# A periodic drain in the scatter queue of a fused attention and mixture-of-experts kernel

## The chip, the cores and the metric

The kernel runs on one core of one Trainium2 chip. The metric is the device time of one execution in microseconds. Three runs of the kernel before took 1343.55, 1356.92 and 1354.8 us; their median is 1354.8 us.

## What is computed

The input is x of shape (4, 512, 256), 2048 rows of 256 floats. Four residual layers follow each other, each on a layernorm of its input:

```
x = x + attn_a(layernorm(x))     # 32 query heads of 8, 8 key/value heads, rope, causal
x = x + ffn(layernorm(x))        # the layer called "f" in the kernel
x = x + attn_b(layernorm(x))     # differential attention, 16 heads, causal
x = x + ffn(layernorm(x))        # the same weights; the layer called "h"
```

The part that matters is ffn. Each of the 2048 rows goes to a shared expert (width 352) and to 4 of 16 routed experts (width 176):

```
scores  = softmax(xt @ Wg.T)                     # 16 experts
topi    = top 4 experts within the best 2 of 4 groups
h       = silu(xt @ W1[e]) * (xt @ W3[e]);  y = sum over chosen e of score * (h @ W2[e])
z       = (silu(xt @ Ws1.T) * (xt @ Ws3.T)) @ Ws2.T
out     = y + z
```

## The kernel before, in words

**Tiling.** The 2048 rows are 16 tiles of 128 rows (NT = 16). In a ffn layer, DVE works out in two halves of 8 tiles each (the function assign, L1308) which slot of a table in DRAM, x_slots, each (row, choice) pair goes to; its slot numbers are in slot_i. There are 16 x 4 = 64 such pairs of a tile and a choice (NT * TOPK). For each of them, POOL issues one indirect DMA, here called a scatter: 128 rows of 265 floats (the 256 features, the slots, the scores and the row number) go from y_sb to 128 places of x_slots (L687). Scatter n carries tile n // 4, choice n % 4.

**What limits the scatters.** Scatters of even number count their landing on one semaphore, scat0, those of odd number on another, scat1. Before scatter n, POOL waits until scatter n - 2 has landed (L686), so at most two are under way. Scatters 0 to 31 need the first half of the slots, 32 to 63 the second half.

**What waits for the scatters.** Once scatters 0 to 39 have landed (EARLY_T * TOPK = 40; L503 and L504), SyncE starts to load the gathered rows, one tile of 128 slots after another (load, L468), 72 tiles in all (NJ), eight ahead of their use. Before tile 24 it waits for all 64 (L511 to L513). Before that, SyncE itself has filled the ends of the experts' regions with zero rows (16 small DMAs, L498) and has stored x as the start of the accumulator (store_x, L489), three of four batches.

**The expert stage.** PE turns two loaded tiles at a time (turn_in, L1971), multiplies them by the first-layer weights of their experts (L1996), turns the result (L2003) and multiplies by the second-layer weights (L2029 to L2034). ACT and DVE sit between (L896 to L905, L1463, L1471). DVE scales the result into one of eight buffers, yt (L1480), and POOL sends each result back with an indirect DMA that adds to y_f or y_h in DRAM (result_out, L703).

**POOL's order in a ffn layer.** Scatters 0 to 51 stand one after another, with one wait for the second half of the slots before scatter 32. Then come the results of the 72 tiles, and after each of the first six results, two of the last 12 scatters. Everything on POOL is in this written order.

**Beside the scatters.** While the scatters run, PE computes the shared expert (L1938, L1948), with ACT's silu (L896) and DVE's product and sum (L1429, L1421).

Attention, weights and the return of the result (L525 to L534) are not touched.

Of the kernel before, what the change touches and what calls it, by code (L numbers as in the profile page):

```python
# [26 lines left out]
NT = B * TB  # L27
# [26 lines left out]
TOPK = 4  # L54
# [46 lines left out]
def build(nc, ins, out):  # L101
    ctx = ExitStack()
    with ctx:
# [3 lines left out]
        def sem(name):  # L107
            return ctx.enter_context(nc.semaphore(name))
# [159 lines left out]
        def sm(name):  # L268
            if name not in S:
                S[name] = sem(name)  # L270
            return S[name]
# [65 lines left out]
        def past(f, n):  # L337

            return n if f == "h" else 0
# [341 lines left out]
        def pool_ffn(pool, f):  # L681

            def scatter(n):
                t, k = n // TOPK, n % TOPK
                if n >= 2:
                    pool.wait_ge(sm(f"scat{n % 2}"), 16 * (n // 2 + past(f, NT * TOPK // 2)))  # L686
                pool.indirect_dma_start(x_slots, bass.IndirectOffsetOnAxis(ap=slot_i[:, t, k:k + 1], axis=0),  # L687
                                        y_sb[:, t, :], None).then_inc(sm(f"scat{n % 2}"), 16)

            outs = [(j, h) for j in range(NJ) for h in range(1 + (j in MIX))]  # L690

            def scatter_out(s):


                if s >= ACCS:
                    i, h = outs[s - ACCS]
                    if h == 0:
                        pool.wait_ge(sm(f"store{i % XR}"), 16 * (i // XR + 1 + past(f, NJ // XR)))
                    else:
                        pool.wait_ge(sm("store_second"), 16 * (MIX.index(i) + 1 + past(f, MIXED)))  # L700
                j, h = outs[s]
                to = j if h == 0 else NJ + MIX.index(j)
                pool.indirect_dma_start(y_acc[f][s % ACCS], bass.IndirectOffsetOnAxis(ap=dest[:, to:to + 1], axis=0),  # L703
                                        yt[:, j % XR, :], None, compute_op=ALU.add)\
                    .then_inc(sm(f"store{j % XR}" if h == 0 else "store_second"), 16)

            def result_out(j):
                pool.wait_ge(sm("e_dest"), j // 4 + 1 + past(f, NJ // 4))
                pool.wait_ge(sm("e_y_ev"), j + 1 + past(f, NJ))
                if j == 0:  # L710
                    pool.wait_ge(sm("acc_x"), 16 * B * (1 + past(f, 1)))
                scatter_out(outs.index((j, 0)))
                if j in MIX:
                    scatter_out(outs.index((j, 1)))

            pool.wait_ge(sm("e_slots"), 1 + past(f, 2))
            pool.wait_ge(sm("cleared"), 16 * 23)
            for n in range(TH * TOPK):
                scatter(n)
            pool.wait_ge(sm("e_slots"), 2 + past(f, 2))  # L720
            for n in range(TH * TOPK, EARLY_T * TOPK + LATE_FIRST):
                scatter(n)
            late = range(EARLY_T * TOPK + LATE_FIRST, NT * TOPK)
            for j in range(NJ):
                result_out(j)
                for n in late[2 * j:2 * j + 2]:
                    scatter(n)
# [1418 lines left out]
```

## Time and profile before

| what | value |
|---|---|
| median of three runs | 1354.8 us |
| time of the profiled execution | 1349.85 us |
| its span | 1348.1 us |
| PE busy | 1144.7 us (85%) |
| DVE busy | 873.5 us (65%) |
| POOL busy | 689.1 us (51%) |
| ACT busy | 541.6 us (40%) |
| mean granted clock of TensorE, share of full speed | 0.934 |

The span is what the profiler recorded from first to last instruction; the device time of the same execution is 1.75 us longer. A busy share is the mean over all stages, and says little about one stage. Layer f runs its scatters from 388 us on and its experts until about 648 us; layer h from 1037 us and until about 1314 us. All times in the views are counted from the start of the span. "DMA_INDIRECT" on POOL is the time in which POOL makes the descriptors of a scatter; the data moves after it.

### The profile page before, as it was taken

How to read it: one execution, taken by the hardware profiler on the slowest of the kernel's cores; microseconds unless marked ns; L12 is line 12 of the kernel's file. 1: busy time of each engine (PE TensorE's matmuls, PEld its weight loads, DVE VectorE, ACT ScalarE, POOL GpSimd, SP SyncE). 2: the span in 40 equal slices, each digit the busy share in tenths (PEclk: the TensorE clock that was granted, in tenths of full speed). 3: DMA queues.
4: the chain of work that ended last, by engine and by line, in shares of the span. 5: the costliest groups of instructions: out<-in, count | busy, mean ns of one | idle time of the engine just before them, and what ended most of it. 6: DMA issues, size and time to landing. Idle time of an engine off the chain costs nothing.

```text
span 1348.1 us, 26055 instructions
## 1 busy us (share of the span) xinstructions
PE 1144.7 (85%) x8706; PEld 614.0 (46%) x8706; DVE 873.5 (65%) x2067; ACT 541.6 (40%) x846; POOL 689.1 (51%) x841
## 2 busy tenths in 40 slices
PE   6888999998899699999288899999779859999990
PEld 2343444342655366566154344444246435665650
DVE  5688899981576145555388899999568523554543
ACT  2124777779431122222032577777844001222210
POOL 4452344544036577767552454545521652787671
PEclk9897999999889799999699899999988978999995
DMA  4424433320825479987754321221062345898868
GB/s 144 144 86 126 122 109 121 106 64 2 287 72 149 150 183 164 158 156 113 192 178 143 108 61 53 62 50 50 3 255 48 113 129 144 168 159 161 153 91 262
DMA packets 145875, 169.84 MB, mean 126 GB/s; under 512 B 20240, under 2 KB 130768, under 8 KB 145232
## 3 DMA queue, kind: packets, MB, share of 16 engines
q1 hardware_dynamic: 115856, 128.79, 32.7%
q0 software_dynamic: 29184, 38.36, 16.7%
q8 instruction: 73, 1.20, 0.4%
q10 hardware_dynamic: 704, 1.02, 0.2%
q14 instruction: 58, 0.48, 0.1%
HBM read 93.29 MB, written 76.18 MB: 126 GB/s over the span
## 4 chain that ended last, share of the span: by engine, by line
PE 57%; DVE 18%; issue 6%; DMA 6%; ACT 6%; POOL 2%; SPq 2%; another core or an unknown queue 1%; POOLq 0%; ACTq 0%; DVEq 0%
PE pair_ps L1996 11%; PE o_ps L1761 9%; ACT arena L849 4%; DVE nm L1123 4%; PE pair_ps L2029 4%; DMA x_slots<-y_sb,slot_i 3%; DVE bm L1123 3%; PE pair_ps L2032 2%; PE t_ps L1787 2%; PE pair_ps L1711 2%; PE pair_ps L1592 2%; PE pair_ps L1691 2%; PE pair_ps L1716 2%; PE pair_ps L2003 2%; PE pair_ps L1686 2%
## 5 line engine op out<-in xcount | busy, mean ns | idle before, releaser
L849 ACT ACTIVATE arena<-pair_ps 128x1024 f32<-128x1024 f32 x320 | 322.9, 1024 | 130.6 <-PE pair_ps L1686 75.9
L625 POOL TENSOR_SCALAR_AFFINE_SELECT arena<-arena 128x512 f32<-128x512 f32 (+1 forms) x320 | 175.0, 547 | 241.4 <-ACT arena L849 240.9
L1123 DVE TENSOR_REDUCE nm<-pair_ps 128x2 f32<-128x1024 f32 (+1 forms) x192 | 232.6, 1222 | 33.4 <-PE pair_ps L1735 29.5
L687 POOL DMA_INDIRECT x_slots<-y_sb,slot_i x128 | 123.6, 966 | 168.0 <-DVE slot_i L1321 94.0
L1761 PE MATMUL o_ps<-arena 128*9 128x512 f32 (+7 forms) x2048 | 176.8, 440 | 4.2 <-POOL arena L625 4.1
L1996 PE MATMUL pair_ps<-arena 128*128 x512 | 168.6, 471 | 2.5 <-ACT arena L900 2.5
L1123 DVE TENSOR_REDUCE bm<-pair_ps 128x8 f32<-128x1024 f32 x128 | 155.3, 1217 | 4.1 <-PE pair_ps L1735 1.0
L703 POOL DMA_INDIRECT y_h<-xnT,dest x80 | 125.3, 1567 | 58.6 <-DVE xnT L1480 31.4
L703 POOL DMA_INDIRECT y_f<-xnT,dest x80 | 124.6, 1558 | 42.0 <-issue 21.2
L1463 DVE TENSOR_TENSOR arena<-arena,pair_ps 128x128 f32<-128x128 f32 x144 | 41.4, 288 | 116.6 <-ACT arena L905 77.1
L1996 PEld LDWEIGHTS pair_ps<-arena 128*128 128x128 f32 x512 | 93.8, 195 | 43.9 <-issue 6.3
L905 ACT ACTIVATE arena<-pair_ps 128x176 f32<-128x176 f32 x144 | 45.5, 317 | 138.6 <-PE pair_ps L1996 86.9
L1480 DVE TENSOR_SCALAR xnT<-pair_ps,slot_w 128x256 f32<-128x256 f32 x144 | 64.9, 481 | 45.5 <-PE pair_ps L2034 15.9
L1938 PE MATMUL pair_ps<-arena 128*128 128x512 f32 (+1 forms) x192 | 90.3, 614 | 0.0
L1735 PE MATMUL pair_ps<-c_b 64*128 64x128 bf16 (+1 forms) x1280 | 85.0, 210 | 0.0
L1735 PEld LDWEIGHTS pair_ps<-c_b 64*128 64x128 bf16 x1280 | 60.8, 98 | 33.5 <-issue 4.2
L1711 PE MATMUL pair_ps<-arena 48*128 48x512 bf16 x256 | 51.2, 394 | 22.7 <-ACT arena L849 17.9
L896 ACT ACTIVATE sil<-pair_ps 128x512 f32<-128x512 f32 (+1 forms) x24 | 14.3, 595 | 128.3 <-PE pair_ps L1938 66.3
L1686 PE MATMUL pair_ps<-arena 51*128 51x512 bf16 x256 | 51.2, 395 | 15.3 <-DVE bm L1123 7.3
L1761 PEld LDWEIGHTS o_ps<-arena 128*9 128x9 f32 (+1 forms) x2048 | 38.9, 93 | 53.3 <-issue 30.7
L2029 PE MATMUL pair_ps<-arena 128*128 x224 | 59.5, 388 | 0.5 <-DVE arena L1471 0.5
L900 ACT ACTIVATE arena<-t_ps 128x512 f32<-128x512 f32 x36 | 21.5, 597 | 86.2 <-PE t_ps L1971 73.8
(275 smaller groups left out, 2012.8 us busy)
## 6 DMA issues: line engine op xcount, KB each, us to landing
arena<-x_slots SPq DMA_DIRECT2D x128, 132.5 KB
arena<-in_w SPq DMA_DIRECT2D x4, 2816.0 KB, 18.9
arena<-q_a SPq DMA_DIRECT2D x64, 96.0 KB
arena<-q_b SPq DMA_DIRECT2D x64, 96.0 KB
y_f<-hw SPq DMA_DIRECT2D x11, 512.0 KB, 2.9
y_h<-hw SPq DMA_DIRECT2D x11, 512.0 KB, 2.9
arena<-in_w SPq DMA_DIRECT2D x2, 2048.0 KB, 17.4
arena<-y_f SPq DMA_DIRECT2D x8, 512.0 KB
```

The source lines that it names most:

```text
L625: pool.affine_select(p, p, pattern, ALU.is_ge, 0.0, base=0, channel_multiplier=-1)\
L687: pool.indirect_dma_start(x_slots, bass.IndirectOffsetOnAxis(ap=slot_i[:, t, k:k + 1], axis=0), y_sb[:, t, :], None).then_inc(sm(f"scat{n ...
L703: pool.indirect_dma_start(y_acc[f][s % ACCS], bass.IndirectOffsetOnAxis(ap=dest[:, to:to + 1], axis=0), yt[:, j % XR, :], None, compute_op ...
L849: act.activation(p_ring[:, U % RING, :], pair_ps[:, pair_at("T", n, u)].rearrange("p a c -> p (a c)"), ACT.Exp, scale=SCALE).then_inc(sm(" ...
L1123: dve.tensor_reduce(dst, src, X, ALU.max, negate=not 2 <= u < 4).then_inc(sm("t_max_done"), 1)
L1686: mm = pe.matmul(ps, k_of(s, g, h, KM, 0, P), q_of(g, h, KM, 0, T), start=True, stop=True, skip_group_check=True)
L1711: pe.matmul(ps, q_of(g, h, KQ, 3 * P, T), k_of(s, g, h, KQ, 0, T), start=True, stop=False, skip_group_check=True)
L1735: mm = pe.matmul(blocks[:, :, 64 * half:64 * half + 64], mask_h[lo:lo + 64, half * P:half * P + P], ident_b[lo:lo + 64, lo:lo + 64].unsque ...
L1761: mm = pe.matmul(o_ps[32 * h:32 * h + vw, T - c:T], v_all[:, g, TB * b + j, v0:v0 + vw], p_ring[:, U % RING, a:a + c], start=j == 0, stop= ...
L1938: mm = pe.matmul(st_ps[0:m, k % 2, 512 * a:512 * a + 512], ws13[:, a, e, r:r + m], xnT_all[:, e, b * T:(b + 1) * T], start=e == 0, stop=e ...
L1996: mm = pe.matmul(s_ps[:, j % 2, 0:2 * INTER], xgT[:, j // 2 % 2, j % 2, c, :], w13[:, c, ds(e, 1), :].rearrange("p a i -> p (a i)"), start ...
L2029: pe.matmul(st_ps[:, h, 512:512 + E], hsT[:, h, :], w2[:, 0, ds(e, 1), :].rearrange("p a d -> p (a d)"), start=True, stop=False, skip_grou ...
```

## The change

Before scatters 8, 16, 24, 32, 40, 48 and 56 of each ffn layer, POOL also waits until the scatter just before has landed. So nothing of the scatters is under way when one of these is issued. That is 7 waits in each of the two layers. No instruction is added on another engine, no data moves differently, and POOL's order stays the same.

```diff
                 t, k = n // TOPK, n % TOPK
                 if n >= 2:
                     pool.wait_ge(sm(f"scat{n % 2}"), 16 * (n // 2 + past(f, NT * TOPK // 2)))
+                if n > 0 and n % 8 == 0:
+                    pool.wait_ge(sm(f"scat{(n - 1) % 2}"), 16 * ((n + 1) // 2 + past(f, NT * TOPK // 2)))
                 pool.indirect_dma_start(x_slots, bass.IndirectOffsetOnAxis(ap=slot_i[:, t, k:k + 1], axis=0),
                                         y_sb[:, t, :], None).then_inc(sm(f"scat{n % 2}"), 16)
```

For n = 8, scatters 1, 3, 5 and 7 count on scat1, and (8 + 1) // 2 = 4 landings are asked for: all of them.

## Rows read from the trace of the kernel before

**Rows 1.** The page's chain of work that ended last: shares by line.

```profile
PE pair_ps L1996 11%; PE o_ps L1761 9%; ACT arena L849 4%; DVE nm L1123 4%; PE pair_ps L2029 4%; DMA x_slots<-y_sb,slot_i 3%; DVE bm L1123 3%; PE pair_ps L2032 2%; PE t_ps L1787 2%; PE pair_ps L1711 2%; PE pair_ps L1592 2%; PE pair_ps L1691 2%; PE pair_ps L1716 2%; PE pair_ps L2003 2%; PE pair_ps L1686 2%
```

**Rows 2.** The chain in layer f: start us, us, what.

```profile
430.03 4.93 DMA x_slots<-y_sb,slot_i
...
437.95 5.19 DMA x_slots<-y_sb,slot_i
...
451.84 2.67 DMA x_slots<-y_sb,slot_i
454.52 0.03 SPq L504
...
465.06 2.66 DMA arena<-x_slots
...
467.82 0.44 PE t_ps L1971 x2
```

**Rows 3.** POOL's timeline, layer f: scatters 8, 9, 12, 16, 17, 24, 25, 32, 33.

```profile
401.89 0.95 POOL L687 DMA_INDIRECT x_slots<-y_sb,slot_i  x1 [2.21 <-DMA x_slots<-y_sb,slot_i]
403.15 0.96 POOL L687 DMA_INDIRECT x_slots<-y_sb,slot_i  x1 [0.30 <-issue]
...
407.48 0.96 POOL L687 DMA_INDIRECT x_slots<-y_sb,slot_i  x1 [0.64 <-DMA x_slots<-y_sb,slot_i]
...
413.60 0.96 POOL L687 DMA_INDIRECT x_slots<-y_sb,slot_i  x1 [0.69 <-issue]
415.06 0.96 POOL L687 DMA_INDIRECT x_slots<-y_sb,slot_i  x1 [0.50 <-issue]
...
425.60 0.96 POOL L687 DMA_INDIRECT x_slots<-y_sb,slot_i  x1 [0.52 <-DMA x_slots<-y_sb,slot_i]
427.30 0.96 POOL L687 DMA_INDIRECT x_slots<-y_sb,slot_i  x1 [0.74 <-DMA x_slots<-y_sb,slot_i]
...
439.76 0.96 POOL L687 DMA_INDIRECT x_slots<-y_sb,slot_i  x1 [0.86 <-DMA x_slots<-y_sb,slot_i]
443.40 0.96 POOL L687 DMA_INDIRECT x_slots<-y_sb,slot_i  x1 [2.68 <-DMA x_slots<-y_sb,slot_i]
```

**Rows 4.** SyncE's waits in 380 to 480 us: total, times, longest.

```profile
SPq L504 <- DMA x_slots<-y_sb,slot_i: 16.0, 1, 16.0
```

**Rows 5.** Windows in layer f: busy us of each engine, granted clock, DMA share, GB/s.

```profile
455.00:460.00 5.00, 1.23 (x4) 0.58 (x4) 0.00 (x0) 0.00 (x0) 3.52 (x4) 0.50 0.55 160
460.00:465.00 5.00, 3.90 (x8) 2.29 (x8) 1.20 (x7) 0.91 (x2) 2.81 (x4) 0.50 0.76 219
```

**Rows 6.** Timelines, layer f: last scatter and first result on POOL, tile 24's load on SyncE.

```profile
474.84 1.61 POOL L703 DMA_INDIRECT y_f<-xnT,dest  x1 [2.29 <-issue]
...
500.60 0.96 POOL L687 DMA_INDIRECT x_slots<-y_sb,slot_i  x1 [0.30 <-issue]
...
508.74 1.39 SPq L468 DMA_DIRECT2D arena<-x_slots  x2
```

**Rows 7.** POOL's waits in 470 to 650 us: total, times, longest.

```profile
POOL y_f L703 <- DVE xnT L1480: 13.0, 12, 2.4
```

**Rows 8.** Timelines, layer h: SyncE, then POOL (scatter 41, first result), PE, ACT.

```profile
1057.02 41.42 SPq L498 DMA_DIRECT2D x_slots<-x_slots  x16
1101.34 11.24 SPq L489 DMA_DIRECT2D y_h<-x_sb  x3
...
1098.58 0.96 POOL L687 DMA_INDIRECT x_slots<-y_sb,slot_i  x1 [0.64 <-DMA x_slots<-y_sb,slot_i]
...
1138.69 1.62 POOL L703 DMA_INDIRECT y_h<-xnT,dest  x1 [19.89 <-DVE xnT L1480]
...
1092.00 2.05 PE L1948 MATMUL t_ps<-arena,hw 128*128 128x256 f32 x4 [18.12 <-DVE x_sb L1421]
...
1124.60 0.63 PE L1971 MATMUL t_ps<-c_f,arena 128*128 128x128 f32 x4 [1.81 <-issue]
...
1084.62 0.60 ACT L896 ACTIVATE sil<-pair_ps 128x512 f32<-128x512 f32 x1 [18.63 <-issue]
```

## The prediction

> **What bounds the kernel now.** I read the page's chain of waits first. PE work has the largest shares, and the scatters of the dispatch hold 3% of the span [rows 1]. That is enough to ask where they stand. The same chain in order of time answers it: between 388 and 455 us nearly every link is a scatter or POOL's issue of the next, and the last of them, scatter 39, leaves at 451.84 and lands 2.67 us later. SyncE is released at 454.52, its loads follow, and the experts' chain on PE begins with a load that lands at 467.7 [rows 2]. SyncE's waits say the same: it had done its own work 16.0 us before and stood at L504 for the scatters alone [rows 4]. PE is idle meanwhile: 1.23 of 5 us busy in 455 to 460, 3.90 of 5 in the next window, at the lower level of its clock (0.50 granted, 1.2 GHz) in both [rows 5]. So in layer f, what delays scatter 39 delays everything after it.
>
> In layer h the same scatters end nothing. Scatter 41 starts at 1098.58, released by the landing of 39, so 39 had landed by then. SyncE issues its three stores until 1101.34 + 11.24 = 1112.6, loads then, and PE turns the first tile at 1124.60 when its shared expert is done [rows 8]. The slack is 1112.6 - 1098.6 = 14 us at SyncE.
>
> **The change, part by part.** The added wait makes scatter n leave when n - 1 has landed, and not n - 2. Where before scatter n + 1 was held by exactly that landing, its own start tells when n could go now. From the starts [rows 3]:
> - n = 8: 403.15 - 401.89 = 1.26 us later at most. Scatter 9 left after 0.96 us of descriptors and a 0.30 us pause, the shortest spacing in the rows, so it was not held. Scatter 7 had landed by then; the price is 0 to 1.26, and I take 0.6.
> - n = 16: 415.06 - 413.60 = 1.46 us.
> - n = 24: 427.30 - 425.60 = 1.70 us.
> - n = 32: 443.40 - 439.76 = 3.64 us, behind the long landing of scatter 31 (5.19 us, [rows 2]).
>
> That is what the even scatter loses. The odd one behind it can now follow at the shortest spacing, 1.26 us, and loses just that; its loss at n = 32 is 443.40 + 1.26 - 443.40 = 1.26 as well. Scatter 39 is odd and is the one waited for. Its loss before any recovery is 0.6 + 3 x 1.26 = 4.4 us.
>
> Recovery: pairs that leave 1.26 us apart turn round a little faster than pairs evenly spaced. From scatter 8 to 12, started in close pairs, a pair took (407.48 - 401.89) / 2 = 2.8 us; from 16 to 24, evenly spaced, (425.60 - 413.60) / 4 = 3.0 us [rows 3]. With 0.2 us for some three pairs behind each of the two drains that break an even spacing (16 and 24), 1.2 us come back. **Layer f, start of the experts: 4.4 - 1.2 = about +3.2 us.** PE's clock adds nothing: it is already at 0.50 across the whole idle stretch [rows 5], and a longer idle leaves it there.
>
> The bounds: below, 0 for each drain, if the landing of n - 1 comes in fact right behind that of n - 2; the long landings (4.93 and 5.19 us, rows 2) may also be due to SyncE's stores at that moment and be met by other scatters now. Above, 4 us for each drain, the longest landing of the rows, 5.19 us, with a 0.26 us release in place of the 1.45 us pace: 16 us in all.
>
> **Drains 40 and 48** lie behind the point that SyncE waits for. What stands behind them on POOL is scatters to 51, then the results. The first result starts at 474.84 after 2.29 us of idle time [rows 6]. With all six drains scatter 51 is 3.2 + 2 x 1.26 = 5.7 us later, the first result's data 3.2 us later, so POOL's lag of 2.5 us nearly fits in that idle time. What is left is covered by the 13.0 us in which POOL waits for DVE's results later in the stage [rows 7], and by the eight yt buffers. If that cover were gone, the price would be some 1 us.
>
> **Drain 56** stands two results further on, with a result of 1.6 us of POOL's time between scatters 55 and 56; by then 55 has landed or nearly so: 0 to 1 us on POOL, 0 on the end. All 64 scatters are wanted before tile 24's load at 508.74; scatter 63 starts at 500.60 [rows 6] and, with the 2.67 us of a landing, is home at 503.3, 5.4 us ahead. It moves by 5.7 to 7, the load by 3.2, so 1.6 us or more are left.
>
> **Layer h**: four drains, at 4.4 us, fit in 14 us of slack. POOL waits 19.89 us for its first result at 1138.69 [rows 8], so drains 40 and 48 are hidden too. Zero; if the cover of 14 us went, 3.2 us as in f.
>
> The sum is +3.2 us on the profiled execution: 1349.85 + 3.2 = 1353.1 us. That execution is 4.95 us under the median of the runs shown; on the median the same sum is 1358.0. I give the middle of the two, **1355.5 us**. The runs shown lie 13.4 us apart, so a change of this size hardly shows in the time. About 1%, 13.5 us, is what a measurement here can tell from no change.
>
> **The rivals.**
> - *Drains under load, slower.* The drain exposes a whole landing, and the landings beside SyncE's zero rows and stores are the long ones, 4.93 and 5.19 us [rows 2]. If the drains of layer f meet such landings, each costs 4 us: 1349.85 + 16 = 1365.9 us. It passes the 1% where a drain costs over 13.5 / 4 = 3.4 us. For it: two of the long landings are among scatters 27 to 31, right before drain 32. Against it: no scatter from 16 to 25 shows one, and drain 32 pays only once the stall that scatter 33 paid already. The Trainium skill, "DMA: Bandwidth & Descriptors", section "Latency and other measured facts", speaks for this rival: it gives access to HBM 0.2 us on average and 2 us at high load, as the main part of a transfer's fixed cost. By it four loaded drains would cost 4 x 1.8 = 7.2 us more, an estimate from that page; this trace agrees that landings vary (2.67 to 5.19 us), but shows the long ones to be few. Chance 0.10.
> - *The idle gap in layer h shrinks, faster.* ACT starts its silu at 1084.62 after 18.63 us in which nothing that the profile shows held it, and PE stands for 18.12 us until 1092.00 [rows 8]. If this is a fetch of instructions held up behind DMA traffic, a queue emptied now and then might let it through. PE would then end its shared expert up to 18 us sooner. SyncE would not follow that far: its fills are issued until 1057.02 + 41.42 = 1098.4, the stores take 11.24 us more, and a load 2.66 us to land [rows 2, 8], so PE's first turn could come at 1112.3 in place of 1124.60. The most that can be won is 12 us: 1349.85 + 3.2 - 12 = 1341.0 us; with half of it 1347. Against it: between drains the traffic is the same. The Trainium skill, "Runtime: NRT & Kernel Launch", section "Instruction fetch mechanics", says that the sequencers stream their code in blocks by a queue of their own and that this is mostly hidden; by it there would be nothing to win. The trace neither names the 18.63 us a fetch nor excludes it. Chance 0.12.
> - *The waits cost nothing.* The landing of n - 1 comes with that of n - 2, or the stalls are met elsewhere: 1349.9 us. For it: only scatter 8. Chance 0.10.
> - *The forecast*, +1 to +7 us, has the remaining 0.68.
>
> **How the numbers follow.** The range reaches down almost to the second rival's 1341 and up to the first's 1365.9, with a little for the difference of the bases: 1342 to 1367 us. Faster by over 1% needs more than the whole gap's gain or a low draw of the runs: 0.06. Slower by over 1% is the first rival with a little for what I don't see: 0.11. Within 1%: 0.83.
>
> **What would show each step right or wrong.** In the trace after, scatters 8, 16, 24 and 32 of layer f should start about 2.7 us behind the one before, and the next 1.26 us behind. From scatter 0's start to the release at L504 it should take 66.3 + 3.2 = 69.5 us, and PE's first tile should follow as now. SyncE in layer h should still end its stores some 12 us ahead of PE's first turn. The forecast is wrong if drains meet 5 us landings, if the pace between drains changes, if the gap in layer h has another length, or if POOL's lag reaches DVE's result buffers.

## The result

| | changed | before |
|---|---|---|
| median of 20 runs each, same chip | 1363.95 us (1356.88 to 1370.63) | 1351.65 us (1343.55 to 1361.78) |
| ratio, 95% interval | 1.009 (1.0068 to 1.0112) | |
| profiled execution | 1358.44 us | 1349.85 us |
| its span | 1356.7 us | 1348.1 us |

The change costs 12.3 us, 0.9%. That lies within 1%, though the interval reaches 1.12%, and 1363.95 lies within the range of 1342 to 1367. But the sum of the forecast was +3.2 us, and its likeliest case ended at +7. The size was wrong, and what follows is mostly about that. Here and below, medians are over all runs, while a ratio and its interval compare only the runs within 1.5% of the fastest of their kernel, which makes a difference in set 1 alone.

### The profile page after: what moved, and what is told of

Its sections match the earlier page's. It is cut to its first block, busy times and chain, and to the rows that moved or that the text cites. A ratio compares the mean times of both kernels' runs of the same rounds, so it can differ in the third digit from the quotient of the medians.

```text
span 1356.7 us, 26067 instructions
## 1 busy us (share of the span) xinstructions
PE 1144.0 (84%) x8706; PEld 610.8 (45%) x8706; DVE 872.1 (64%) x2067; ACT 542.0 (40%) x846; POOL 691.1 (51%) x841
## 4 chain that ended last, share of the span: by engine, by line
PE 54%; DVE 16%; DMA 12%; ACT 6%; issue 6%; POOL 2%; SPq 2%; another core or an unknown queue 1%; POOLq 0%; ACTq 0%; DVEq 0%
PE pair_ps L1998 11%; PE o_ps L1763 9%; DMA x_slots<-y_sb,slot_i 9%; ACT arena L851 4%; DVE nm L1125 4%; PE pair_ps L2031 4%; DVE bm L1125 3%; PE pair_ps L2034 2%; PE t_ps L1789 2%; PE pair_ps L1713 2%; PE pair_ps L1594 2%; PE pair_ps L2005 2%; PE pair_ps L1693 2%; PE pair_ps L1718 2%; PE pair_ps L1688 2%
## 5 line engine op out<-in xcount | busy, mean ns | idle before, releaser
L851 ACT ACTIVATE arena<-pair_ps 128x1024 f32<-128x1024 f32 x320 | 323.1, 1025 | 131.2 <-PE pair_ps L1688 76.5
L1482 DVE TENSOR_SCALAR xnT<-pair_ps,slot_w 128x256 f32<-128x256 f32 x144 | 65.0, 481 | 46.2 <-PE pair_ps L2036 14.6
L1713 PE MATMUL pair_ps<-arena 48*128 48x512 bf16 x256 | 51.6, 397 | 22.6 <-ACT arena L851 18.4
L1973 PE MATMUL t_ps<-c_f,arena 128*128 128x128 f32 x144 | 25.2, 295 | 36.5 <-DMA arena<-x_slots 36.5
```

What stands on the lines that cost most here:

```text
L851: act.activation(p_ring[:, U % RING, :], pair_ps[:, pair_at("T", n, u)].rearrange("p a c -> p (a c)"), ACT.Exp, scale=SCALE).then_inc(sm(" ...
L1713: pe.matmul(ps, q_of(g, h, KQ, 3 * P, T), k_of(s, g, h, KQ, 0, T), start=True, stop=False, skip_group_check=True)
```

## The profile after

The chain of waits on the profile's page gives the first hint. The scatters had 3% of the span in it [rows 1] and now have 9%:

```profile
PE pair_ps L1998 11%; PE o_ps L1763 9%; DMA x_slots<-y_sb,slot_i 9%; ACT arena L851 4%; DVE nm L1125 4%; PE pair_ps L2031 4%; DVE bm L1125 3%; PE pair_ps L2034 2%; PE t_ps L1789 2%; PE pair_ps L1713 2%; PE pair_ps L1594 2%; PE pair_ps L2005 2%; PE pair_ps L1693 2%; PE pair_ps L1718 2%; PE pair_ps L1688 2%
```

9% of 1357 us is some 120 us, and the scatters to number 39 of one layer take 70. So they now end the time in both layers, where before it was layer f alone. (Lines from 687 on have moved by two.)

POOL's timeline of the changed kernel in layer f: start, duration, and in brackets the idle time ahead. The rows are scatters 8, 16 to 18, 20, 24, 26, 30, 32, 39 and 51, and the first result. They answer to [rows 3] and [rows 6].

```profile
400.59 0.96 POOL L689 DMA_INDIRECT x_slots<-y_sb,slot_i  x1 [2.49 <-DMA x_slots<-y_sb,slot_i]
...
414.60 0.96 POOL L689 DMA_INDIRECT x_slots<-y_sb,slot_i  x1 [2.78 <-DMA x_slots<-y_sb,slot_i]
415.87 0.96 POOL L689 DMA_INDIRECT x_slots<-y_sb,slot_i  x1 [0.30 <-issue]
417.60 0.96 POOL L689 DMA_INDIRECT x_slots<-y_sb,slot_i  x1 [0.77 <-DMA x_slots<-y_sb,slot_i]
...
420.88 0.96 POOL L689 DMA_INDIRECT x_slots<-y_sb,slot_i  x1 [1.05 <-DMA x_slots<-y_sb,slot_i]
...
428.92 0.96 POOL L689 DMA_INDIRECT x_slots<-y_sb,slot_i  x1 [2.55 <-DMA x_slots<-y_sb,slot_i]
...
433.44 0.96 POOL L689 DMA_INDIRECT x_slots<-y_sb,slot_i  x1 [2.30 <-DMA x_slots<-y_sb,slot_i]
...
441.93 0.96 POOL L689 DMA_INDIRECT x_slots<-y_sb,slot_i  x1 [3.41 <-DMA x_slots<-y_sb,slot_i]
...
446.59 0.96 POOL L689 DMA_INDIRECT x_slots<-y_sb,slot_i  x1 [2.43 <-DMA x_slots<-y_sb,slot_i]
...
456.42 0.96 POOL L689 DMA_INDIRECT x_slots<-y_sb,slot_i  x1 [0.30 <-issue]
...
476.02 0.96 POOL L689 DMA_INDIRECT x_slots<-y_sb,slot_i  x1 [2.41 <-DMA x_slots<-y_sb,slot_i]
...
482.76 1.62 POOL L705 DMA_INDIRECT y_f<-xnT,dest  x1 [0.30 <-issue]
```

Each drain is there: scatters 8, 16, 24, 32 wait 2.4 to 2.8 us. The pace before scatter 16 does not break, but its start is 414.60 - 410.86 = 3.74 us behind scatter 15, which left at 410.86. The chain of waits says what these 3.74 us are (start, us, what):

```profile
410.86 2.97 DMA x_slots<-y_sb,slot_i
...
413.87 0.73 issue
```

Scatter 15 takes 2.97 us to land, and POOL then needs another 0.73 us in which the profile shows nothing that it waits for. All four drains of layer f have these 0.73 us. Behind the long landings of the kernel before it was 0.26 us: 437.95 + 5.19 = 443.14, and scatter 33 starts at 443.40 [rows 2, 3]. Scatters 26 and 30, which have no drain, wait long too (2.30 and 3.41 us): the two stalls that before met scatters 29 and 33 now meet others. From scatter 0's start (388.27 before, 386.59 after) to scatter 39 it takes 69.8 us in place of 63.6.

POOL's waits from 380 us to scatter 51, total, times and longest, after and then before:

```profile
POOL x_slots L689 <- DMA x_slots<-y_sb,slot_i: 37.4, 27, 3.4
```

```profile
POOL x_slots L687 <- DMA x_slots<-y_sb,slot_i: 26.6, 33, 2.8
```

The waits put down to a landing add up to 10.8 us more. From scatter 0 to scatter 51 it takes 94.9 us in place of 83.3, so six drains cost 11.6 us, 1.9 us each. SyncE's wait at L504 in layer f, 16.0 us before [rows 4], and the same in layer h, where before it never stood for a scatter:

```profile
SPq L504 <- DMA x_slots<-y_sb,slot_i: 22.1, 1, 22.1
...
SPq L504 <- DMA x_slots<-y_sb,slot_i: 24.7, 1, 24.7
```

On PE, the second turn of a pair of slot tiles (L2003 before, L2005 now) marks each of the 36 pairs of a layer. These are pairs 0 and 9 of layer f, before:

```profile
469.16 0.54 PE L2003 MATMUL pair_ps<-c_f,arena 128*128 128x128 f32 x3 [0.90 <-issue]
...
513.16 0.49 PE L2003 MATMUL pair_ps<-c_f,arena 128*128 128x128 f32 x3
```

and after, with two stalled ones between:

```profile
473.35 0.54 PE L2005 MATMUL pair_ps<-c_f,arena 128*128 128x128 f32 x3 [0.90 <-issue]
...
494.21 0.49 PE L2005 MATMUL pair_ps<-c_f,arena 128*128 128x128 f32 x2 [1.09 <-DVE arena L1465]
...
514.42 0.50 PE L2005 MATMUL pair_ps<-c_f,arena 128*128 128x128 f32 x2 [1.17 <-DVE arena L1465]
...
524.01 0.49 PE L2005 MATMUL pair_ps<-c_f,arena 128*128 128x128 f32 x3
```

These nine pairs take 50.7 us after and 44.0 before; the other 26 take 131.2 to 131.6 us in every kernel here. So the experts start late and then run slowly for nine pairs. This second loss is one that the forecast had put at nothing. What causes it in this trace is not shown. The profile puts no wait of DVE between 470 and 530 us down to the landing of a result, so nothing in it points at the result buffers. The chain of waits runs instead through stretches whose releaser the profile does not know, the longest of them this one:

```profile
504.39 4.88 another core or an unknown queue
```

It ends with ACT's copy of a turn that PE had finished at 504.83 (first PE's row, then ACT's):

```profile
504.17 0.66 PE L1973 MATMUL t_ps<-c_f,arena 128*128 128x128 f32 x4
```

```profile
509.29 0.60 ACT L902 ACTIVATE arena<-t_ps 128x512 f32<-128x512 f32 x1 [4.90 <-remote]
```

ACT takes up ready work 4.5 us late here. Set 1 has the same in layers without the drains that could explain it.

In layer h, POOL's scatter 0 and 39, SyncE's stores and its first load, and PE's first turn now stand so (to be held against [rows 8]):

```profile
1048.48 1.06 POOL L689 DMA_INDIRECT x_slots<-y_sb,slot_i  x1 [46.14 <-DVE slot_i L1323]
...
1120.97 0.96 POOL L689 DMA_INDIRECT x_slots<-y_sb,slot_i  x1 [0.32 <-DMA x_slots<-y_sb,slot_i]
...
1090.50 8.24 SPq L489 DMA_DIRECT2D y_h<-x_sb  x3
...
1124.29 1.49 SPq L468 DMA_DIRECT2D arena<-x_slots  x2
...
1126.88 0.66 PE L1973 MATMUL t_ps<-c_f,arena 128*128 128x128 f32 x2 [17.93 <-DMA arena<-x_slots]
```

The idle gap of 18 us in the shared expert is gone, the stores are out at 1098.7, and the load now waits for scatter 39. PE waits 17.93 us for it. The two profiled executions then add up like this; each row is worked out from the starts of scatter 0 and of pairs 0 and 9 in both traces.

| where the 8.6 us of the profiles arise | us |
|---|---|
| layer f starts earlier (386.59 against 388.27) | -1.7 |
| f, scatter 0 to pair 0: 86.8 against 80.9 | +5.9 |
| f, nine pairs: 50.7 against 44.0 | +6.7 |
| f's pair 9 to h's scatter 0 | +0.6 |
| h, scatter 0 to pair 0: 89.1 against 95.9 | -6.8 |
| h, nine pairs: 48.2 against 44.3 | +3.9 |

Whether the waits brought back the 6.8 us in layer h, the experiments had to tell.

## The experiments

Three sets, each on one chip; kernels of a set share their runs of the kernel before. That kernel's medians show how chips differ: 1360.57 us (1342.76 to 1385.03) in set 1, 1331.65 us (1326.12 to 1337.11) in set 2, 1329.78 us (1324.29 to 1335.04) in set 3. Ratios are compared inside a set. Each diff is against the changed kernel, unless it says otherwise.

### Set 1: which layer, which drains, and four scatters under way

f_only keeps the waits of layer f:

```diff
-                if n > 0 and n % 8 == 0:
+                if f == "f" and n > 0 and n % 8 == 0:
```

> The seven drains stand in layer f alone, layer h is as before. Theory A (drain chain plus POOL's lag): layer f alone pays about 6 us at the release of L504 (scatter 39 starts 69 to 70 us after scatter 0, before 63.6) and some 6 us more in the first nine pairs of tiles, where DVE waits for one of the eight result buffers because POOL began its results late. So +10 to +13 us on the median, nearly all of the +12.3 us of the whole change. Rival B (layer h carries it): layer f pays the +3.2 us of the forecast and the rest of the +12.3 came from layer h, so this kernel stands at +2 to +4 us. Rival C (the idle gap of PE in layer h only fell differently): no steady difference, within 2 us of before.

h_only keeps those of layer h (`if f == "h" and ...` in the same place):

> The seven drains stand in layer h alone. Theory A: what they cost depends on the idle stretch of PE in the shared expert. Where that stretch of some 18 us is there, SyncE is released by its own stores and the drains before scatter 40 are hidden, 0 us at the release; where it is not, the release moves by 6 to 14 us. POOL's lag adds 3 us where the first results find POOL still scattering. So 0 to +8 us on the median, and little in a run with the gap. Rival B: +8 to +10 us. Rival C: within 2 us of before.

early_only keeps drains 8 to 32 in both layers and leaves out 40, 48 and 56:

```diff
-                if n > 0 and n % 8 == 0:
+                if 0 < n <= 32 and n % 8 == 0:
```

> Only the drains at 8, 16, 24 and 32 stay, in both layers. Theory A: scatter 39 of layer f starts 5 to 6 us later than before, and PE's first tile with it; scatter 51 moves by the same 5 to 6 us, so POOL's lag behind PE does not grow, and the first nine pairs of tiles take as long as before (the pair starts 4.8 to 5.6 us apart, none of 6 to 8). The whole is +5 to +7 us from layer f plus 0 to 3 from h. Rival (the gate carries it all): as slow as the whole change, +10 to +13 us. Rival C: within 2 us.

four_in_flight has none of the waits, and lets four scatters be under way. Against the kernel before:

```diff
-                if n >= 2:
-                    pool.wait_ge(sm(f"scat{n % 2}"), 16 * (n // 2 + past(f, NT * TOPK // 2)))
+                if n >= 4:
+                    pool.wait_ge(sm(f"scat{n % 4}"), 16 * (n // 4 + past(f, NT * TOPK // 4)))
...
-                                        y_sb[:, t, :], None).then_inc(sm(f"scat{n % 2}"), 16)
+                                        y_sb[:, t, :], None).then_inc(sm(f"scat{n % 4}"), 16)
```

SyncE waits on all four counters; three one-time memset counters are one, to make room for them.

> No drain; four scatters may be under way, on four semaphores, in place of two (two one-time semaphores of the memsets are merged to make room, which moves no work). Theory A says that the pace of the scatters is set by their landings: then scatter 39 starts after about 39 x 1.27 = 50 us in place of 63.6, layer f's release comes 10 to 13 us earlier, and the kernel is 10 to 15 us faster. Rival D (the pace is POOL's own or the DMA engines' throughput): the landings get longer by as much as more of them overlap, and the time is within 3 us of before.

| set 1 | median us | ratio | interval |
|---|---|---|---|
| f_only | 1368.96 | 0.9992 | 0.9926 to 1.0057 |
| h_only | 1362.85 | 1.003 | 0.998 to 1.008 |
| early_only | 1355.83 | 0.9998 | 0.996 to 1.0035 |
| four_in_flight | 1425.86 | 1.0533 | 1.047 to 1.0595 |

On this chip no share of the drains costs anything that can be told, though the intervals of the first two reach +0.6% and +0.8%. Over all runs the medians are 8.4 and 2.3 us above and 4.7 us below that of the kernel before, from runs that spread over 20 to 42 us. Removing the waits costs 5%, where 10 to 15 us had been expected to be won. The traces suggest why the terms don't show. In every layer that has drains (f_only f, h_only h, both of early_only) the shared expert runs through. In each that has none (f_only h, h_only f) there is the gap of 15 to 20 us that layer h of the kernel before has. This is PE, then ACT, in layer f of h_only:

```profile
436.93 2.04 PE L1950 MATMUL t_ps<-arena,hw 128*128 128x256 f32 x4 [15.49 <-DVE x_sb L1423]
```

```profile
428.43 0.60 ACT L898 ACTIVATE sil<-pair_ps 128x512 f32<-128x512 f32 x1 [16.40 <-remote]
```

So in layers alike in everything but the waits, pair 0 comes 85.4 us (drained) and 92.0 us (gap) after scatter 0 in layer f, and 84.5 and 106.6 in layer h. In layers with neither, on the chip of set 2, it is 80 to 81 us. So four drains take 4 to 5 us there and a gap 11 to 26 us, and a change that adds the one and prevents the other can come out at nothing. Each of these is a single trace, and that of f_only is the longest of its 12 runs.

early_only's expectation failed in one part. Without drains 40 and 48 its first nine pairs should have taken 44 us, and they take 54.9 in layer f and 46.2 in layer h. They are slow in the undrained layers too: 50.6 (h_only f), 49.4 (f_only h), 51.5 and 54.0 us (four_in_flight). On this chip the second loss of the profile after thus comes without the drains as well.

four_in_flight has the gap at its largest, with the scatters at the shortest pace (scatter 39 49.9 us after scatter 0, POOL never waiting for a landing). POOL's waits from 380 to 456 us, then PE and ACT:

```profile
POOL x_slots L687 <- issue: 15.6, 51, 0.3
```

```profile
456.83 2.05 PE L1948 MATMUL t_ps<-arena,hw 128*128 128x256 f32 x4 [46.67 <-DVE x_sb L1421]
```

```profile
432.88 0.60 ACT L896 ACTIVATE sil<-pair_ps 128x512 f32<-128x512 f32 x1 [36.18 <-issue]
...
460.56 0.60 ACT L896 ACTIVATE sil<-pair_ps 128x512 f32<-128x512 f32 x1 [27.08 <-remote]
```

PE stands idle 46.7 us in layer f, the stores behind the shared expert end 102.4 us after scatter 0, and pair 0 follows at 123.2 us. The scatters were done 50 us earlier and it helped nothing.

The prediction had allowed that the gap is a fetch of instructions. The profile's queues speak against it: between 396 and 448 us of h_only, a window that holds all of ACT's 16.4 us, no queue of the kind "instruction" moved a packet; there are only these two (packets, MB, share of 16 engines). ACT's gap in layer h of the kernel before (1066 to 1085 us) has none either.

```profile
q0 software_dynamic: 1635, 4.62, 25.2%
q1 hardware_dynamic: 742, 1.32, 11.6%
```

And DVE is held as well, in the same stretch, on its own results: these waits are too short to be marked where there is no gap. First DVE in layer f of h_only, then the same operations in the kernel before on the chip of set 2.

```profile
417.31 0.21 DVE L1394 TENSOR_SCALAR scratch<-scratch 128x1 f32<-128x1 f32 x1 [1.18 <-DVE scratch L1393]
...
418.82 0.16 DVE L1397 TENSOR_TENSOR scratch<-scratch 128x1 f32<-128x1 f32 x1 [0.80 <-DVE scratch L1396]
```

```profile
418.23 0.21 DVE L1392 TENSOR_SCALAR scratch<-scratch 128x1 f32<-128x1 f32 x1
...
418.98 0.16 DVE L1395 TENSOR_TENSOR scratch<-scratch 128x1 f32<-128x1 f32 x1
```

Not all of the idle time is lateness. In h_only, PE had made ACT's input by 421.3, so ACT's silu at 428.43 is 7.1 us late. DVE then adds into x_sb, whose input was there:

```profile
435.38 0.75 DVE L1423 TENSOR_TENSOR x_sb<-x_sb,t_ps 128x256 f32<-128x256 f32 x2 [5.62 <-remote]
```

That is another 5.6 us. PE follows DVE at once, so it only waits. So two engines are late in taking up ready work, while POOL issues scatters without a drain. In layer f of four_in_flight the two are 22.7 and 21.1 us late. That is all the profile shows of the cause.

### Set 2: the price of the drains where there is no gap

control is the kernel before under another name, and after_again the changed kernel. gate_40_48 keeps two drains:

```diff
-                if n > 0 and n % 8 == 0:
+                if n in (40, 48):
```

four_drain is four_in_flight with the drain added: all three scatters under way have landed before every eighth. Against four_in_flight:

```diff
+                if n > 0 and n % 8 == 0:
+                    for m in range(n - 3, n):
+                        pool.wait_ge(sm(f"scat{m % 4}"), 16 * (m // 4 + 1 + past(f, NT * TOPK // 4)))
```

> The kernel before, unchanged, as a second profile of it and as the measure of how far two sets of runs of one kernel lie apart. All theories: a ratio of 1 within its interval. Theory E (dense scatters hold up the other engines, drains prevent it): at least one of the two ffn layers shows the idle stretch of PE, 15 to 20 us long, ended by DVE's add into x_sb behind a late silu of ACT. Rival C (the stretch is chance and has nothing to do with the drains): present or absent like in any other kernel.

> The changed kernel, unchanged, on the chip of this set. Theory E: the idle stretch is absent in both layers, the runs lie closer together than those of the kernel before, and the time is that of a layer without the stretch plus the drains: on a chip where the kernel before often shows the stretch twice, the two kernels lie within 5 us of each other or the changed one is faster; where it shows it seldom, the changed one is 10 us slower. Theory A alone (drains cost, nothing is given back): +12 us again.

> Only the drains at 40 and 48 stay, in both layers. Theory A (POOL's lag): scatter 39 starts as before (58 to 64 us after scatter 0), scatter 51 leaves 25 us after 39 and not 20, POOL begins its results 3 to 5 us later against PE, and the first nine pairs of tiles take 48 to 51 us and not 44. So +4 to +6 us for each layer that has no idle stretch. Theory E: with no drain before scatter 40 the idle stretch is there in at least one layer. Rival (the drains before 40 carry the loss): no difference within 2 us.

> Four scatters under way as in the slow kernel with four, and a drain before every eighth that waits for all three before it. Theory E (the other engines are held up while POOL issues scatters without a pause): a pause of 2 to 3 us in every 12 us lets them go on, the idle stretch of 27 to 47 us vanishes or falls under 10 us, scatter 39 starts 60 to 65 us after scatter 0, and the kernel is at 1345 to 1365 us where four without drains took 1426. Rival F (four in flight fill the DMA engines or the queue, pause or not): the stretch stays above 20 us and the time above 1400 us.

| set 2 | median us | ratio | interval | against before |
|---|---|---|---|---|
| control | 1332.23 | 1.0001 | 0.9982 to 1.002 | +0.6 |
| after_again | 1352.42 | 1.0151 | 1.0123 to 1.0179 | +20.8 |
| gate_40_48 | 1337.38 | 1.004 | 1.0021 to 1.0058 | +5.7 |
| four_drain | 1328.06 | 0.9972 | 0.9951 to 0.9993 | -3.6 |

control shows the kernel before without a gap in either layer, and gate_40_48, which has no drain ahead of scatter 40, has none either. The expectations of both had called for a gap in at least one layer, so a lack of drains alone does not bring it. four_drain has none as well, but here that says nothing of what its drains prevent. Layer h of control, by the same rows as above:

```profile
1035.45 1.05 POOL L687 DMA_INDIRECT x_slots<-y_sb,slot_i  x1 [46.94 <-DVE slot_i L1321]
...
1099.62 0.96 POOL L687 DMA_INDIRECT x_slots<-y_sb,slot_i  x1 [0.40 <-DMA x_slots<-y_sb,slot_i]
...
1076.23 9.76 SPq L489 DMA_DIRECT2D y_h<-x_sb  x3
...
1103.00 1.49 SPq L468 DMA_DIRECT2D arena<-x_slots  x2
...
1105.52 0.66 PE L1971 MATMUL t_ps<-c_f,arena 128*128 128x128 f32 x2 [9.32 <-DMA arena<-x_slots]
```

The stores are out at 1086.0 and SyncE waits for the scatters; there are no 14 us of slack. This is the case in which the change costs most, +1.5%. From scatter 0 to the first load it takes 66.1 us in control's layer f and 72.5 in after_again's (+6.4), in h 67.5 and 72.2 (+4.7). Nine pairs take 43.1 us in both layers of control, 47.3 and 47.7 in after_again (+4.2, +4.6). The sum is 19.9 us, for 20.8 measured.

after_again had been expected at +10 to +12 us and costs 20.8, since both losses appear in both layers.

gate_40_48 has only the second of the two losses: its first load comes at 66.6 and 65.8 us (+0.5 and -1.7 against control), and nine pairs take 45.8 and 46.5 us, 2.7 and 3.5 more. That makes 6.2 us, or 5.0 with the first loads, for 5.7 measured. The path of this loss stands in DVE's waits between 470 and 530 us, for control, after_again and gate_40_48 (total, times, longest):

```profile
DVE xnT L1480 <- DMA y_f<-xnT,dest: 0.4, 1, 0.4
```

```profile
DVE xnT L1482 <- DMA y_f<-xnT,dest: 7.2, 4, 3.6
```

```profile
DVE xnT L1482 <- DMA y_f<-xnT,dest: 7.3, 5, 3.1
```

POOL issues the results behind scatter 51. If scatter 51 is late the first results are late, DVE finds its result buffers still to be read, and PE's pairs wait for DVE. This path is shown for set 2; in the profile after, on the chip of the result, layer f has no such wait.

### Set 3: fewer and more drains, and a pause in place of a wait

early_again is early_only on this chip. every4 has a drain before every fourth scatter (`n % 4 == 0`). four_drain16 is four_drain with `n % 16 == 0`. four_pause is four_in_flight with a pause of POOL in place of the wait, by four memsets of a tile that nobody else uses, each waited for:

```diff
+                if n > 0 and n % 8 == 0:
+                    for i in range(4):
+                        pool.memset(idle[:], 0.0).then_inc(sm("m_chain"), 1)
+                        pool.wait_ge(sm("m_chain"), 24 + n // 8 * 4 - 3 + i + past(f, 24 + 28))
```

> The drains at 8, 16, 24 and 32 alone, in both layers, a second time, since the first set stood on a chip where the kernel before often shows the idle stretch of PE. Where the kernel before shows none, theory A gives the release 6.4 us later in f and 4.6 in h and no longer first nine pairs (43 to 44 us): +10 to +12 us. With the drains at 40 and 48, whose own kernel took +5 us, that adds up to about the +20 us of the whole change on such a chip. If the drains and POOL's lag are not separate, this kernel takes +15 us or more. Where the kernel before shows the stretch in some runs, the difference shrinks to 0 to +8 us.

> Twice the drains: before every fourth scatter, 15 in each layer instead of 7; nine lie before scatter 40. Theory A: each costs the same 1.2 to 1.6 us, so scatter 39 starts 9 x 1.2 to 9 x 1.6 = 11 to 14 us later than without, 74 to 77 us after scatter 0, and POOL's lag adds 8 to 10 us to the first nine pairs in each layer: +35 to +45 us against the kernel before where this shows no idle stretch. Rival G (a drain costs most where it breaks an even rhythm, and more drains find no rhythm to break): under +28 us. No idle stretch in either layer.

> Four under way, a drain of all before every sixteenth scatter only. Theory E says how long POOL may go without a pause before the other engines are held up: the stretch in the kernel with four and no drain began some 10 us after scatter 0, ACT's silu number 3 and DVE behind it. If 16 scatters without a pause (20 us) are too many, the stretch is back, 5 to 15 us long, at silu number 3, and scatter 39 still starts earlier, 54 to 57 us after scatter 0; the time is 0 to 25 us above the kernel with a drain every eighth. If they are not, the release comes 3 to 4 us earlier in each layer and the kernel is 5 to 8 us faster than the one with a drain every eighth, 8 to 12 us faster than before.

> Four under way and no drain; in place of it, before every eighth scatter POOL clears a small tile four times (512 floats in each partition, about 3 us in all), while landings go on unwatched. No result depends on that tile. Theory E1 (what frees the other engines is that POOL issues no scatter for some 3 us): the idle stretch of 27 to 47 us vanishes or falls under 10 us, and the time is within 15 us of the kernel with a drain every eighth. Theory E2 (the wait for the landing itself matters, for example since it bounds what is queued): the stretch stays above 20 us and the time above 1390 us.

| set 3 | median us | ratio | interval | against before |
|---|---|---|---|---|
| early_again | 1342.47 | 1.0098 | 1.007 to 1.0125 | +12.7 |
| every4 | 1370.92 | 1.0323 | 1.0285 to 1.036 | +41.1 |
| four_drain16 | 1314.73 | 0.9887 | 0.9853 to 0.992 | -15.1 |
| four_pause | 1327.56 | 0.9982 | 0.9964 to 1.0 | -2.2 |

early_again costs 12.7 us, and the same kernel cost nothing in set 1. Its first load is at 73.3 and 71.3 us (+7.2, +3.8 over control, which ran on the chip of set 2), its nine pairs take 43.1 and 44.8: the first loss almost alone. With gate_40_48's 5.7 us that makes 18.4 of after_again's 20.8. DVE waits 1.2 us for results' DMAs between 470 and 530 us, where after_again had 7.2.

every4 doubles the drains, and the price doubles: first load at 82.4 and 81.2 us (+16.3, +13.7), nine pairs +6.4 and +6.5, 42.9 us in all for 41.1 measured. Nine drains lie ahead of scatter 39, so one costs 16.3 / 9 = 1.8 or 13.7 / 9 = 1.5 us. DVE waits 8.5 us for results:

```profile
DVE xnT L1482 <- DMA y_f<-xnT,dest: 8.5, 3, 4.7
```

four_drain16, in four runs, is 15.1 us faster than the kernel before; 8 to 12 had been expected, and the changed kernel was not run on this chip. POOL's scatters 15, 16 and 32 in layer f:

```profile
405.38 0.96 POOL L690 DMA_INDIRECT x_slots<-y_sb,slot_i  x1 [0.30 <-issue]
408.66 0.96 POOL L690 DMA_INDIRECT x_slots<-y_sb,slot_i  x1 [2.32 <-DMA x_slots<-y_sb,slot_i]
...
432.72 0.96 POOL L690 DMA_INDIRECT x_slots<-y_sb,slot_i  x1 [4.13 <-DMA x_slots<-y_sb,slot_i]
```

Between drains scatters leave 1.26 us apart; with the three longer waits (the third, before scatter 48, is 3.98 us) scatter 51 starts 74.2 us after scatter 0, and 82.3 us in control. Its first load comes at 59.1 and 59.6 us (-7.0 and -7.9 against control), nine pairs take 43.1 and 44.8, and PE has no gap. That is -13.2 us for -15.1 measured.

four_pause has a pause of 2.29 us of memsets before every eighth scatter, and no gap. That would say that the landing itself need not be waited for. But no trace from this chip has a gap, and four_in_flight was not run on it, so whether any pause is needed here is open.

## Why the prediction was wrong in its size

**What bounds the kernel: right for the profile, too narrow for the kernel.** Layer f is bound by the scatters, as read. That layer h has slack was true of the one execution profiled, because its gap of 18.12 us [rows 8] held the stores back. Where it is absent (set 2), the drains cost 4.7 us at the load and 4.6 us in the nine pairs. The zero for layer h was a step that failed: it took a disturbance for a property of the stage. The rows were there to ask it of: 18.63 us "issue" in layer h, and nothing like it in layer f, which runs the same code.

**Release of layer f: priced 3.2, measured 5.9 to 6.4 us.** The direction was right, the sizes were not. The sign named was a drained scatter about 2.7 us behind the one before, which is the landing alone. Measured are 3.4 to 3.7 us, since 0.73 us follow the landing. From scatter 0 on, drain 8 costs 0.4 us, drain 16 and drain 24 cost 1.9 and 1.6 (from the odd scatter before to the odd one behind), and the stretch from scatter 25 to 33, with drain 32 in it and two long stalls in both kernels, 1.6. That is 5.5 us where 4.4 had been priced. The recovery of 1.2 us did not occur: the pairs behind drain 16 start at 414.60, 417.60 and 420.88, 3.0 and 3.3 us apart, no faster than even ones, and behind drains 8 and 16 another 0.7 us are lost. On the chips of sets 2 and 3 a drain ahead of scatter 39 costs 0.9 to 1.8 us.

**Drains 40 and 48: priced 0, at most 1 us, measured 2.7 and 3.5 us a layer in gate_40_48.** POOL's idle time of 2.29 us [rows 6] was there, and is used up (0.30 ahead of 482.76). But POOL came 3.2 us later to scatter 39 by the forecast and 6.3 us in fact, and drains beside the loads cost more: from scatter 39 to 51 it takes 25.1 us in place of 19.8. The first result left 7.9 us later (482.76 against 474.84), PE's pair 0 4.2 us later. Lateness of this kind reaches DVE's result buffers in set 2. On the chip of the result the nine pairs lose 6.7 us in layer f and 3.9 in layer h, and the profile does not tie the 6.7 us to these buffers; in layer h DVE waits 1.2 us for them. How much of these losses is the drains' stays open. The 13.0 us of POOL waiting for DVE [rows 7] covered nothing, since those waits lie in another part of the stage. Of drain 56 alone no run tells.

**The rivals.** *Drains under load* named the right side and the wrong price, 4 us where at most 1.9 are paid. *The gap shrinks* happened beside the forecast and not in its place: -6.8 us in the profile of layer h, and perhaps in set 1 enough to cancel the drains. *The waits cost nothing* is refuted by sets 2 and 3. The change's price is thus best read as two opposite terms, 20.8 us against whatever part of the gaps it prevents. The median's +12.3 us lies between what set 1 and set 2 show. That the range and the 1% held is luck: the upper bound of 1367 came from a rival with a chance of 0.10, and the time stayed below it because the credit in layer h, forecast at zero, offset errors of the other sign.

**What stays open.** That drains prevent the gap rests on few traces. In set 1 there is none in four drained layers, and one in both undrained layers and both of four_in_flight. In the two profiles of the result layer f has none with or without drains, and layer h has one without. What holds ACT and DVE up is not shown, nor which is first: in the three gap layers with two scatters under way, scatter 39 starts 58.0 to 58.4 us after scatter 0, and in undrained layers without a gap 62.2 to 64.2 us, so the denser scatters may be cause or result. four_drain16 was not run on a chip where the gap appears; whether it is better there too is not known.

## What to carry to other kernels

Price a wait that empties a short queue by the landing it exposes and the time from there to the next issue (0.73 us here), less the pace it replaces, count on no recovery, and follow the lateness past the waited-for point, to the next queue behind the same engine. Before a stage is given slack, look whether its other half was merely disturbed in the profiled execution: compare two stages that run the same code. Where DMAs are issued one by one with two under way, more under way with a rare drain can be worth more than the waits' position: here 1.1%.

## What the runs showed of the hardware

- A scatter of 128 rows leaves POOL every 1.26 us when nothing holds it (0.96 of descriptors, 0.30 idle). With two under way it was held to some 1.5 to 1.6 us a scatter. Emptying the queue cost 0.9 to 1.9 us each time ahead of scatter 39, and 2.1 and 2.4 us for each of the drains at 40 and 48 (gate_40_48 against control). After such a drain POOL started 0.73 us behind the landing.
- In some layers without drains, ACT and DVE took up ready work late (by 7.1 and 5.6 us in h_only, 22.7 and 21.1 us in four_in_flight), and PE stood idle behind them 15 to 20 us in one piece with two scatters under way, 46.7 us with four. It was seen on the chips where the kernel before took 1350 to 1360 us, and in no trace of those where it took 1330.
- The same kernel's median differed by 2.3% between chips (1329.78 to 1360.57 us), and the same change measured +0.9% on one and +1.5% on another.
